# A hand-ordered transformer kernel: value products and scores side by side on TensorE, the sum of p ahead of the scaling of o on VectorE

## The chip, the cores and the metric

One core of a Trainium2 chip runs the whole program. Time is the device time of that core in microseconds (us). The core's engines work from queues of their own and meet only at semaphores: TensorE (PE; PEld is its weight load), VectorE (DVE), ScalarE (ACT), GpSimd (POOL) and SyncE (SP), which only issues DMAs.

## The reference, cut to what matters

```python
x = x + tanh(g_xattn) * xattn(layernorm(x), ctx)              # once, 4 x 512 tokens of 128
x = x + tanh(g_ffn) * body(layernorm(x))
def body(x):
    for i in range(6):
        q, k, v = split(shift_tokens(x) @ Wqkv[i])            # 16 heads of 64
        q, k = rotary(l2norm(q) * q_scale), rotary(l2norm(k) * k_scale)
        sim = q @ k.T * 8, masked to windows of 32 (own and the one before)
        p = exp(sim - max(sim));  o = (p @ v) / sum(p)
        x = o @ Wo[i] + x
        x = (a * gelu(gate)) @ W2[i] + b2[i] + x              # a, gate from layer_norm(shift_tokens(x)) @ W1[i] + b1[i]
    return x
```

All of it is float32.

## The kernel before, in words

After a start of some 50 us (cross attention) the kernel runs the six layers as 192 *units*. A unit is one tile of 128 tokens and one half of the heads (eight heads, 512 columns); eight units make a *group* (one batch element of one layer), four groups a layer, 24 groups in all. The order on each engine is written out by hand as a loop `for n in range(SLOTS)`. A *slot* is one pass n of this loop, `g = n // 8`, `s = n % 8`, and every engine has its own list of steps for a slot, each for an older or newer unit: `queries_keys(n)` beside `scores(n - 3)` and `attend(n - 5)`. So the steps of a unit are spread over seven slots, and the feed-forward work of a group over the slots of the next two groups (`if s == ...`).

TensorE, in a slot: `queries_keys(n)` (L376, q and k of a unit into one of two double banks), `attend(n - 5)` (L448, the value products p v), `values(n)` (L389, v), `transpose_o(n - 6)` (L461), `scores(n - 3)` (L423), `transpose_p(n - 4)` (L436), `transpose_k(n - 2)` (L410), `transpose_q(n - 2)` (L399), and between them by s: `mean` (L498), `fold_bias` (L488, only in the first group of a layer, at s = 2), `variance` (L507), the `up` products (L516), `project_out` (L472, at s = 2 and 6), `down` (L527, at s = 7). `attend` and `scores` consist of 16 small products each, four windows by four pairs of heads, with 32 columns of the array apiece (`tile_position=(0, 32 w)`); every other product uses 128 columns. In the trace a float32 product is two pieces, so such a group is 32 pieces; a transpose is one piece.

Results go to three PSUM banks in turn, the ring: each product calls `turn()` when it is emitted, takes the next bank, and waits until the reader of three turns earlier is done (`ring_read`). So the order in which TensorE's steps stand also sets whose reader each of them waits for. q and k have banks of their own, and so have the scores. `queries_keys(n)` waits for `qn_done` of unit n - 2, which `scale_q(n - 2)` on VectorE gives in the same slot n.

VectorE, in a slot: `sum_p(n - 5)` (L880, the row sums of p), `newton(n - 2)` (L837, L840, L842: three instructions on 128x16, the inverse norms of q and k), `scale_k` (L850) and `scale_q` (L858) of n - 2, `maxima(n - 4)` (L865), `invert_sum(n - 5)` (L888), `less_maxima(n - 4)` (L873), a step by s (among them `centre` at s = 1, L923), `sum_squares(n - 1)` (L824), `clamp_squares(n - 1)` (L830), further steps by s (`add_attention` and `rstd_newton` at s = 3, L907 to L940), `scale_o(n - 5)` (L898, which reads the value products), and after it `layer_norm` (L947, at s = 3, on which the `up` products wait) and `finish` (L978, at s = 1, only for the last four groups).

GpSimd turns k and q of a unit by the rotary tables: six instructions on 128x512 (L1053, L1060, L1096 for k, then L1053, L1060, L1089 for q), started by `scale_k`. ScalarE squares q and k, takes exponentials and copies the ring's banks: v, o, p, k, q (L627, L690, L680, L654, L645). SyncE copies v of a unit into `vw`, once for each window, in eight or ten DMAs, behind the value products of two units before.

Of the kernel before, what the change touches and what calls it, by code (L numbers as in the profile page):

```python
# [66 lines left out]
def build(nc, x_in, ctx_in, g_xattn, g_ffn, Wq, bq, Wk, bk, Wv, bv, Wo_x, bo, Wqkv, q_scale, k_scale,  # L67
          Wo, ln_g, ln_b, W1, b1, W2, b2, rope_in, mats_in, mask_in, out):
    ctx = ExitStack()
    with ctx:  # L70
# [211 lines left out]
        def _(pe):  # L282
# [77 lines left out]
            def queries_keys(u):  # L360
                if not 0 <= u < UNITS:
                    return
                g, layer, b, t, half = place(u)
                if u % UPG == 0 and layer == 0:
                    pe.wait_ge(xT_ready, 2 * (b + 1))
                if u == 1:
                    pe.wait_ge(xT_ready, 4)
                if u % UPG == 0 and layer > 0:
                    pe.wait_ge(*evicted("down", g - B))
                if u % (UPG * B) == 0:  # L370
                    pe.wait_ge(w_dma, 16 * 2 * (1 + B * layer))
                pe.wait_ge(qn_done, past(u - 1))
                tok = xT[:, b, t * P:(t + 1) * P]
                for i in range(2):
                    cut = i * INNER + half * UW
                    mm = pe.matmul(QK[u % 2][:, i * UW:(i + 1) * UW], tok, wqkv[:, layer % 2, cut:cut + UW],  # L376
                                   start=True, stop=True)
                mm.then_inc(qk_mm, 1)
# [60 lines left out]
            def attend(u):  # L439
                if not 0 <= u < UNITS:  # L440
                    return
                i = turn("pv", u)
                pe.wait_ge(vw_dma[u % 2], vw_count(u))
                pe.wait_ge(ring_read[i % RINGS], i // RINGS)
                pe.wait_ge(*evicted("p", u))
                for k in range(HP):
                    for w in range(NW):
                        mm = pe.matmul(heads(RING[i % RINGS][WIN * w:WIN * (w + 1), k * P:(k + 1) * P]),  # L448
                                       pT[:, u % 2, k, WIN * w:WIN * (w + 1)],
                                       vw[:, u % 2, w, :, k * DH:(k + 1) * DH], start=True, stop=True,  # L450
                                       tile_position=(0, WIN * w))
                mm.then_inc(ring_made[i % RINGS], 1)
# [88 lines left out]
            for n in range(SLOTS):  # L541
                g, s = n // UPG, n % UPG
                queries_keys(n)
                attend(n - 5)
                values(n)
                transpose_o(n - 6)
                scores(n - 3)
                transpose_p(n - 4)
                if s == 0:
                    mean(g - 2)  # L550
                if s == 2:
                    fold_bias(g - 2)
                if s == 3:
                    up("gate", 1, g - 2, 0)
                    up("gate", 1, g - 2, 2)
                transpose_k(n - 2)
                if s == 1:
                    variance(g - 2)
                if s == 2:
                    project_out(g - 1, 0)  # L560
                if s == 3:
                    up("gate", 1, g - 2, 1)
                    up("a", 0, g - 2, 0)
                if s == 4:
                    up("a", 0, g - 2, 2)
                if s == 5:
                    up("a", 0, g - 2, 1)
                if s == 6:
                    project_out(g - 1, 1)
                if s == 7:  # L570
                    down(g - 2)
                if s == 0:
                    transpose_out(g - 3)
                transpose_q(n - 2)
# [179 lines left out]
        def _(dve):  # L754
# [225 lines left out]

            for n in range(SLOTS):
                g, s = n // UPG, n % UPG
                sum_p(n - 5)
                newton(n - 2)
                scale_k(n - 2)
                scale_q(n - 2)
                maxima(n - 4)
                invert_sum(n - 5)
                less_maxima(n - 4)
                if s == 1:  # L990
                    centre(g - 2)
                if s == 2:
                    add_eps(g - 2)
                if s == 3:
                    add_bias(g - 2)
                if s == 5:
                    gated(g - 2, 2)
                if s == 6:
                    gated(g - 2, 1)
                sum_squares(n - 1)  # L1000
                if s == 0:
                    add_ffn(g - 3)
                clamp_squares(n - 1)
                if s == 3:
                    add_attention(g - 1, 0)
                    rstd_newton(g - 2)
                if s == 7:
                    add_attention(g - 1, 1)
                if s == 4:
                    gated(g - 2, 0)  # L1010
                scale_o(n - 5)
                if s == 3:
                    layer_norm(g - 2)
                if s == 1:
                    finish(g - 3)


        @block.gpsimd
# [238 lines left out]
```

## Time and profile before

| | |
|---|---|
| median of 3 runs | 1823.83 us (1823.41 to 1828.24) |
| the profiled execution | 1824.23 us, span 1822.2 us |
| granted TensorE clock, mean | 0.99 of full speed |
| TensorE busy | 1750.3 us, 96% |
| TensorE weight load busy | 1116.2 us, 61% |
| VectorE busy | 1619.0 us, 89% |
| ScalarE busy | 1327.5 us, 73% |
| GpSimd busy | 1500.4 us, 82% |
| chain that ended last | TensorE 77%, VectorE 13%, GpSimd 5% |

The busy share of TensorE counts pieces whose ends are modelled; how long a step really holds the engine is read from the start of one group of instructions to the start of the next. An instruction's time includes what it waits inside the engine: a 128x16 instruction that takes 0.17 us at one place and 1.14 us at another did not compute for longer.

### The profile page before, as it was taken

To read this page: it belongs to the slowest core of one execution; us is meant where nothing else is said; L and a number is where in the kernel's file an instruction comes from. 1 tells how busy PE (TensorE), PEld (TensorE's weight loads), DVE (VectorE), ACT (ScalarE), POOL (GpSimd) and SP (SyncE) were. 2 spreads that over 40 slices of the span, in tenths; PEclk is the share of its full clock that TensorE was granted. 3 is DMA by queue.
4 is the path that set the end of the run, shared out by engine and by line. 5 is a ranking of instruction groups with operands and counts; after the bars stand their busy time and mean duration, and the time that the engine had idled before them with its cause. 6 is when DMAs were issued, how large, how long until landed. Compare 5 with 4: busy or idle time off the path is not lost.

```text
span 1822.2 us, 48666 instructions
## 1 busy us (share of the span) xinstructions
PE 1750.3 (96%) x18122; PEld 1116.2 (61%) x18122; DVE 1619.0 (89%) x2782; ACT 1327.5 (73%) x2362; POOL 1500.4 (82%) x1204
## 2 busy tenths in 40 slices
PE   7699999999999999999999999999999999999986
PEld 6356666666666666666666666666666666666663
DVE  7799998999999989989999999899999998988874
ACT  3577877877778778778777777787776877877763
POOL 4799888888888888988888888888888888888860
PEclk9999999999999999999999999999999999999998
DMA  4132222222222222322223222222222222222221
GB/s 114 28 87 67 68 71 57 60 73 76 71 63 69 63 66 71 76 65 68 63 56 81 72 70 72 54 63 73 75 72 62 68 58 58 59 71 56 56 64 29
DMA packets 155273, 120.59 MB, mean 66 GB/s; under 512 B 42607, under 2 KB 151457, under 8 KB 154913
## 3 DMA queue, kind: packets, MB, share of 16 engines
q1 hardware_dynamic: 155041, 117.48, 25.1%
q8 instruction: 147, 2.41, 0.6%
q14 instruction: 85, 0.70, 0.1%
HBM read 18.79 MB, written 1.05 MB: 11 GB/s over the span
## 4 chain that ended last, share of the span: by engine, by line
PE 77%; DVE 13%; POOL 5%; issue 3%; SPq 1%; ACT 1%; DMA 1%; DVEq 0%; POOLq 0%; ACTq 0%
PE qk_bank L376 17%; PE ring_bank L448 10%; PE ring_bank L472 9%; PE ring_bank L389 8%; PE sc_bank L423 7%; PE ring_bank L516 6%; PE ring_bank L436 4%; PE ring_bank L399 3%; PE ring_bank L527 3%; PE ring_bank L461 3%; PE ring_bank L410 3%; DVE rn L842 2%; DVE step L837 2%; DVE o L898 2%; DVE qkn L858 2%
## 5 line engine op out<-in xcount | busy, mean ns | idle before, releaser
L1053 POOL TENSOR_TENSOR turned<-qkn,tables 128x512 f32<-128x512 f32 x384 | 489.3, 1274 | 209.8 <-DVE qkn L850 201.5
L1060 POOL TENSOR_TENSOR turned<-qkn,tables 128x512 f32<-128x512 f32 x384 | 496.7, 1294 | 0.0
L376 PE MATMUL qk_bank<-wqkv,xT 128*128 128x512 f32 x768 | 366.5, 600 | 18.8 <-DVE qkn L858 18.6
L1089 POOL TENSOR_TENSOR turned<-turned 128x512 f32<-128x512 f32 x192 | 255.0, 1328 | 15.1
L1096 POOL TENSOR_TENSOR turned<-turned 128x512 f32<-128x512 f32 x192 | 245.1, 1277 | 15.1
L448 PEld LDWEIGHTS ring_bank<-vw,pT 128*32 128x32 f32 x6144 | 156.6, 110 | 143.8 <-issue 143.7
L654 ACT ACTIVATE kB<-ring_bank 64x512 f32<-64x512 f32 x384 | 225.3, 587 | 23.5 <-PE ring_bank L410 21.2
L824 DVE TENSOR_REDUCE ss<-sq 128x16 f32<-128x1024 f32 x192 | 232.0, 1208 | 6.8 <-ACT sq L618 6.8
L627 ACT ACTIVATE vs<-ring_bank 128x512 f32<-128x512 f32 x192 | 114.7, 598 | 163.1 <-PE ring_bank L389 153.4
L898 DVE TENSOR_TENSOR o<-ring_bank,rr 128x512 f32<-128x512 f32 x192 | 132.1, 688 | 104.2 <-PE ring_bank L448 101.3
L389 PE MATMUL ring_bank<-wqkv,xT 128*128 128x512 f32 x384 | 216.1, 645 | 1.6 <-DVE x L978 1.6
L664 ACT ACTIVATE sc_bank<-mask_f 128x512 f32<-128x512 f32 x192 | 114.5, 596 | 136.0 <-DVE pr L873 135.6
L448 PE MATMUL ring_bank<-vw,pT 128*32 128x128 f32 x6144 | 208.4, 276 | 0.1
L423 PE MATMUL sc_bank<-kB,qT 128*32 128x128 f32 x6144 | 207.5, 276 | 0.3
L376 PEld LDWEIGHTS qk_bank<-wqkv,xT 128*128 128x128 f32 x768 | 131.2, 191 | 121.7 <-issue 93.4
L618 ACT ACTIVATE sq<-qk_bank 128x1024 f32<-128x1024 f32 x192 | 198.0, 1031 | 0.0
L423 PEld LDWEIGHTS sc_bank<-kB,qT 128*32 128x32 f32 x6144 | 156.0, 109 | 34.7 <-issue 34.7
L472 PE MATMUL ring_bank<-oT,wo 128*128 128x256 f32 x768 | 173.8, 379 | 0.0
L461 PEld LDWEIGHTS ring_bank<-ident,o 128*128 128x128 f32 x768 | 95.5, 141 | 102.1 <-issue 83.9
L472 PEld LDWEIGHTS ring_bank<-oT,wo 128*128 128x128 f32 x768 | 142.2, 190 | 18.1 <-DVE uT L956 0.8
L516 PE MATMUL ring_bank<-xnT,w 128*128 128x512 f32 x288 | 143.3, 609 | 8.5 <-DVE xnT L947 7.3
L850 DVE TENSOR_TENSOR qkn<-qk_bank,rn 128x512 f32<-128x512 f32 x192 | 132.9, 692 | 20.7 <-DVE rn L842 0.9
(169 smaller groups left out, 3129.3 us busy)
## 6 DMA issues: line engine op xcount, KB each, us to landing
vw<-vs SPq DMA_DIRECT2D x1152, 64.0 KB, 2.1
vw<-vs SPq DMA_DIRECT2D x672, 32.0 KB, 1.9
wqkv<-in_L_ffn_Wqkv_dram SPq DMA_DIRECT2D x20, 384.0 KB, 3.5
wo<-in_L_ffn_Wo_dram SPq DMA_DIRECT2D x20, 128.0 KB, 3.3
w<-in_L_ffn_W_dram SPq DMA_DIRECT2D x6, 341.0 KB, 3.4
wqkv<-in_L_ffn_Wqkv_dram SPq DMA_DIRECT2D x1, 1536.0 KB, 9.5
x<-in_x_dram SPq DMA_DIRECT2D x2, 512.0 KB, 4.7
out_dram<-x SPq DMA_DIRECT2D x4, 256.0 KB, 2.3
```

The costliest lines, as they stand in the source:

```text
L376: mm = pe.matmul(QK[u % 2][:, i * UW:(i + 1) * UW], tok, wqkv[:, layer % 2, cut:cut + UW], start=True, stop=True)
L389: pe.matmul(RING[i % RINGS][:, :], xT[:, b, t * P:(t + 1) * P], wqkv[:, layer % 2, cut:cut + UW], start=True, stop=True).then_inc(ring_mad ...
L423: mm = pe.matmul(heads(SC_BANK[WIN * w:WIN * (w + 1), k * P:(k + 1) * P]), qT[:, u % 2, k, WIN * w:WIN * (w + 1)], kB[:, HP * half + k, :, ...
L448: mm = pe.matmul(heads(RING[i % RINGS][WIN * w:WIN * (w + 1), k * P:(k + 1) * P]), pT[:, u % 2, k, WIN * w:WIN * (w + 1)], vw[:, u % 2, w, ...
L472: mm = pe.matmul(RING[i % RINGS][:, 0:HALF], wo[:, layer % 2, k, :], oT[:, k, HALF * h:HALF * (h + 1)], start=(k == 0), stop=(k == KO - 1))
L516: pe.matmul(RING[i % RINGS][:, :], w1[:, DFF * j + k * P:DFF * j + (k + 1) * P], xnT[:, :], start=True, stop=True).then_inc(ring_made[i % ...
L654: ev = act.activation(kB[64 * h:64 * h + 64, HP * half:HP * half + HP, h, WIN + P * t:WIN + P * t + P], RING[i % RINGS][64 * h:64 * h + 64 ...
L824: dve.tensor_reduce(ss[:, :], heads(sq[:, :]), AX.X, ALU.add).then_inc(ss_done, 1)
L1053: return pool.tensor_tensor(heads(turned[:, u % 2, 2 * i, :]), heads(qkn[:, u % 2, i * UW:(i + 1) * UW]), table.unsqueeze(1).to_broadcast( ...
L1060: return pool.tensor_tensor(halves(turned[:, u % 2, 2 * i + 1, :]), halves(qkn[:, u % 2, i * UW:(i + 1) * UW])[:, :, ::-1, :], table.rearr ...
L1089: pool.tensor_tensor(q, q, turned[:, u % 2, 1, :], ALU.add).then_inc(q_summed, 1)
L1096: pool.tensor_tensor(k, k, turned[:, u % 2, 3, :], ALU.add).then_inc(k_summed, 1)
```

## The change

On TensorE `values(n)` moves ahead of `attend(n - 5)`, and `scores(n - 3)` ahead of `transpose_o(n - 6)`. On VectorE the row sum moves from the start of a slot to the end of the slot before, ahead of `scale_o` (hence `sum_p(n - 4)`), and `finish` from the end of slot s = 1 to a place ahead of `centre`. No instruction is added or removed.

```diff
@@ TensorE, the loop over slots
                 queries_keys(n)
+                values(n)
                 attend(n - 5)
-                values(n)
+                scores(n - 3)
                 transpose_o(n - 6)
-                scores(n - 3)
                 transpose_p(n - 4)
@@ VectorE, the loop over slots
             for n in range(SLOTS):
                 g, s = n // UPG, n % UPG
-                sum_p(n - 5)
                 newton(n - 2)
...
                 less_maxima(n - 4)
                 if s == 1:
+                    finish(g - 3)
                     centre(g - 2)
...
                 if s == 4:
                     gated(g - 2, 0)
+                sum_p(n - 4)
                 scale_o(n - 5)
                 if s == 3:
                     layer_norm(g - 2)
-                if s == 1:
-                    finish(g - 3)
```

TensorE in slot 4 of a group, from q and k on. Before (x16 are the small products of 32 columns):

```order
L376 MATMUL qk_bank<-wqkv,xT 128x512 x2
L448 MATMUL ring_bank<-vw,pT 32x128 x16
L389 MATMUL ring_bank<-wqkv,xT 128x512
L461 MATMUL ring_bank<-ident,o 128x128 x4
L423 MATMUL sc_bank<-kB,qT 32x128 x16
L436 MATMUL ring_bank<-ident,pr 128x128 x4
L410 MATMUL ring_bank<-ident,turned 128x128 x4
```

And in the changed kernel:

```order
L376 MATMUL qk_bank<-wqkv,xT 128x512 x2
L389 MATMUL ring_bank<-wqkv,xT 128x512
L448 MATMUL ring_bank<-vw,pT 32x128 x16
L423 MATMUL sc_bank<-kB,qT 32x128 x16
L461 MATMUL ring_bank<-ident,o 128x128 x4
L436 MATMUL ring_bank<-ident,pr 128x128 x4
L410 MATMUL ring_bank<-ident,turned 128x128 x4
```

The two groups of 32-column products, which had v and o between them, now stand together.

VectorE at the end of slot 3 and the start of slot 4, before (rstd is the normaliser's inverse deviation, xnT its output):

```order
L938 TENSOR_TENSOR dsq<-dsq,xnT 128x512
L940 SCALAR_TENSOR_TENSOR rstd<-dsq,rstd 128x512
L898 TENSOR_TENSOR o<-ring_bank,rr 128x512
L947 SCALAR_TENSOR_TENSOR xnT<-dT,cols,rstd 128x512
L880 TENSOR_REDUCE rs<-pr 128x8
L837 SCALAR_TENSOR_TENSOR step<-seed 128x16
```

And in the changed kernel:

```order
L938 TENSOR_TENSOR dsq<-dsq,xnT 128x512
L940 SCALAR_TENSOR_TENSOR rstd<-dsq,rstd 128x512
L880 TENSOR_REDUCE rs<-pr 128x8
L898 TENSOR_TENSOR o<-ring_bank,rr 128x512
L947 SCALAR_TENSOR_TENSOR xnT<-dT,cols,rstd 128x512
L837 SCALAR_TENSOR_TENSOR step<-seed 128x16
```

The row sum (L880) stood behind layer_norm (L947) and now stands ahead of both it and scale_o (L898).

## Rows read from the trace of the kernel before

**Rows 1.** The page (busy time), and the view of waits, VectorE.

```profile
PE 1750.3 (96%) x18122; PEld 1116.2 (61%) x18122; DVE 1619.0 (89%) x2782; ACT 1327.5 (73%) x2362; POOL 1500.4 (82%) x1204
DVE o L898 <- PE ring_bank L448: 101.3, 100, 3.6
```

**Rows 2.** Timeline, TensorE, slot 0 of group 11: start, us, engine, line, op, operands.

```profile
818.67 1.88 PE L376 MATMUL qk_bank<-wqkv,xT 128*128 128x512 f32 x4
820.48 1.08 PE L448 MATMUL ring_bank<-vw,pT 128*32 128x128 f32 x32
821.49 1.12 PE L389 MATMUL ring_bank<-wqkv,xT 128*128 128x512 f32 x2
822.46 0.60 PE L461 MATMUL ring_bank<-ident,o 128*128 128x128 f32 x4
822.99 1.08 PE L423 MATMUL sc_bank<-kB,qT 128*32 128x128 f32 x32
...
824.49 1.02 PE L498 MATMUL ring_bank<-xT,mean_w 128*128 128x512 f32 x2
825.35 0.60 PE L410 MATMUL ring_bank<-ident,turned 128*128 128x128 f32 x4
...
826.23 1.88 PE L376 MATMUL qk_bank<-wqkv,xT 128*128 128x512 f32 x4
```

**Rows 3.** Timeline, TensorE: starts of slots 2 to 6 and 8; a fold_bias.

```profile
834.33 1.98 PE L376 MATMUL qk_bank<-wqkv,xT 128*128 128x512 f32 x4 [0.39 <-DVE qkn L858]
...
844.58 1.88 PE L376 MATMUL qk_bank<-wqkv,xT 128*128 128x512 f32 x4
...
855.02 1.88 PE L376 MATMUL qk_bank<-wqkv,xT 128*128 128x512 f32 x4
...
862.58 1.88 PE L376 MATMUL qk_bank<-wqkv,xT 128*128 128x512 f32 x4
...
870.81 1.98 PE L376 MATMUL qk_bank<-wqkv,xT 128*128 128x512 f32 x4 [0.52 <-DVE qkn L858]
...
890.33 1.88 PE L376 MATMUL qk_bank<-wqkv,xT 128*128 128x512 f32 x4
...
1055.41 1.40 PE L488 MATMUL ring_bank<-cols,w 128*128 128x1 f32 x12
```

**Rows 4.** Timeline, VectorE and GpSimd, second half of slot 5.

```profile
865.63 0.69 DVE L898 TENSOR_TENSOR o<-ring_bank,rr 128x512 f32<-128x512 f32 x1
...
866.84 1.14 DVE L837 SCALAR_TENSOR_TENSOR step<-seed 128x16 f32<-128x16 f32 x1
...
868.22 1.14 DVE L842 SCALAR_TENSOR_TENSOR rn<-step,seed 128x16 f32<-128x16 f32 x1
869.46 0.69 DVE L850 TENSOR_TENSOR qkn<-qk_bank,rn 128x512 f32<-128x512 f32 x1
...
866.66 1.28 POOL L1060 TENSOR_TENSOR turned<-qkn,tables 128x512 f32<-128x512 f32 x1
868.02 1.30 POOL L1089 TENSOR_TENSOR turned<-turned 128x512 f32<-128x512 f32 x1
870.30 1.27 POOL L1053 TENSOR_TENSOR turned<-qkn,tables 128x512 f32<-128x512 f32 x1 [0.97 <-DVE qkn L850]
```

**Rows 5.** Timeline, VectorE and GpSimd, in slot 2.

```profile
837.63 0.68 DVE L898 TENSOR_TENSOR o<-ring_bank,rr 128x512 f32<-128x512 f32 x1
...
838.82 0.16 DVE L837 SCALAR_TENSOR_TENSOR step<-seed 128x16 f32<-128x16 f32 x1
...
840.49 0.69 DVE L850 TENSOR_TENSOR qkn<-qk_bank,rn 128x512 f32<-128x512 f32 x1
...
838.86 1.28 POOL L1060 TENSOR_TENSOR turned<-qkn,tables 128x512 f32<-128x512 f32 x1
```

**Rows 6.** Timeline, VectorE and TensorE, layer_norm in slot 3.

```profile
849.44 1.05 DVE L947 SCALAR_TENSOR_TENSOR xnT<-dT,cols,rstd 128x512 f32<-128x512 f32 x1
...
850.64 1.96 PE L516 MATMUL ring_bank<-xnT,w 128*128 128x512 f32 x4
```

## Prediction

> **What bounds the kernel now.** I read the page, then TensorE's timeline over one group, then the timelines of VectorE and GpSimd over its tight places. I call one pass of the unit loop a slot, numbered 0 to 7 in a group, and count inside a slot from the start of its q and k product. The page [rows 1] shows three engines nearly full: TensorE at 96%, VectorE at 89%, GpSimd at 82%. VectorE waited 101.3 us for the value products [rows 1], 4.2 us in each of 24 groups: all the slack that it has.
>
> TensorE issues without a gap through slot 0 of group 11 [rows 2]: q and k at 0, value products at 1.81, v at 2.82, o at 3.79, scores at 4.32, then p, mean at 5.82, next slot at 7.56. The slots of the group last 7.56, 8.10, 10.25, 10.44, 7.56, 8.23, then 19.52 for two [rows 2, 3]: 71.66 us, and 24 such groups make nearly the whole time. The start of slot 2 waited 0.39 and that of slot 6 0.52 for VectorE's scaled q (L858) [rows 3]. So TensorE is full except where a loop through VectorE closes late: value products, scale_o, sum_p, newton, scale_k, scale_q, and then the next slot's q and k, which need the bank that scale_q has read. It is this loop that makes slot 1 8.10 and slot 5 8.23 where slots 0 and 4, with as much work for TensorE, take 7.56.
>
> Matmul busy time may mislead, so I put a page's rule against it. The Trainium skill (Perfetto Trace Analysis, Identifying the Most-Contended Engine) judges TensorE by weight loading instead. By that, with 61% [rows 1] against VectorE's 89%, VectorE is the engine to relieve, and an edit that leaves its work unchanged gives nothing. The starts above have no holes to fill, so I keep TensorE as one bound; the rule is rival "same" below.
>
> **TensorE: fewer changes of shape.** Value products and scores use 32 columns of the array, all else 128. One such group spreads its 32 starts over 1.08 less one piece of 0.27, 0.81 us, so 32 steps are 0.83; it holds TensorE for 1.01 [rows 2], so leaving the shape costs 0.18. After it v takes 0.96 where mean, of the same size, takes 0.86: 0.10. Before it q and k take 1.81 where twice 0.86 is 1.72: 0.09. Side by side, the two groups save one entry and one exit: 0.37 a slot, 192 times, 71 us if TensorE bound everywhere. TensorE's own work becomes 7.19 in slots 0, 1, 4, 5; 9.9 in 2 and 6; 9.77 in 3; 8.91 in 7.
>
> **The loop.** v in front delays the value products by 0.86 us. scale_o began 3.05 after the slot's start (862.58, 865.63 [rows 3, 4]); now 3.91, or 4.02 when q and k started late, with the 0.10 that such a start adds. In exchange sum_p leaves the loop. scale_o and sum_p together take 1.19 [rows 5], so 0.60 leaves and 0.86 enters: 0.26 longer, where the loop already decides slots 1 and 5. Its new place is 0.6 us earlier; I take it that the exponentials, which follow the subtracted maxima on ScalarE while VectorE sums squares, are done by then (bounds: nothing, and its own 0.6).
>
> **What else waits in a new order.** The three ring banks are taken in turn, so who waits for whom changes. The value products now take the bank of the k transposes before (ScalarE's copies into kB), and p takes v's bank, so p now waits for ScalarE's copy of v, which itself waits for the copies to vw of four units ago. Those start behind the value products, so 0.86 later in a slot, and VectorE and the SP queue are not otherwise moved. Behind p stand k and q on TensorE. Bounds: nothing, if v is copied in the two microseconds of value products and scores; 0.5 us in slot 1, behind the shortest slot. VectorE decides slot 1 anyway, so nothing. Scores start at 3.52 instead of 4.32, so 0.8 nearer to ScalarE's copy of q, and behind them stand o and p; that could cost up to 0.3 in a slot that follows a Gelu, slot 4. I take nothing and keep 24 x 0.3 = 7 us for the range. o is turned 0.74 later (4.53), two slots' work ahead of its use in the output product.
>
> **The wait behind GpSimd.** newton is three tiny instructions. In slot 5 it lasts from 866.84 to scale_k at 869.46: 2.62 us, with L837 and L842 each 1.14 [rows 4]. Both end just where a GpSimd instruction ends (868.02; 869.3). In slot 2 L837 starts at 838.82, 0.04 before GpSimd's instruction at 838.86; scale_k comes at 840.49, 1.67 us later [rows 5]. So a tiny instruction gets in at once if it comes in the gap between two GpSimd instructions, and otherwise waits for the end of the one that runs: 0.04 ahead of a start it was in time, 0.18 behind one (866.84, 866.66) it was late. Hence everything hangs on newton's phase against GpSimd. The Trainium skill (GPSIMD Engine Reference, Key points) says that the two engines share SBUF interfaces and contend for instructions of two SBUF inputs; the trace agrees, with the 1.14 above.
>
> In a slot whose start waits for VectorE the phases are fixed: scale_k starts 1.35 before the slot (869.46, 870.81), GpSimd's unit 0.51 before it (870.30) [rows 3, 4]. Its fifth instruction then starts 4.53 after the slot's start (838.86 less 834.33) [rows 3, 5]. Before, scale_o ran at 3.30, when VectorE was free, and newton at 4.49: in the gap. Now VectorE would be ready for scale_o at 3.30 + 0.60 = 3.90, but the value products come at 4.02. newton starts at 4.02 + 0.61 = 4.63, 0.10 behind the fifth instruction's start: **it just misses the gap**. Between the two cases seen, 0.04 ahead and 0.18 behind, 0.10 behind is nearer to the late one, so I take that. It then waits for the end of that instruction and for the whole sixth: scale_k comes as in rows 4, 1.44 after the sixth's start (869.46 less 868.02), which is 1.36 after the fifth's [rows 4]: 4.53 + 1.36 + 1.44 = 7.33. The next slot can start at 7.33 + 1.35 = 8.68. In the gap scale_k would come at 840.49 less 834.33 = 6.16 as in rows 5, and the next slot at 7.51.
>
> **Slots of a common group, forecast.** Slot 0: 3.91 + 0.61 + about 1.65 for newton behind one GpSimd instruction + 1.35 = 7.5. Slot 1: 8.7, before 8.1. Slots 2 and 6: TensorE's 9.9 and 0.1 for the late start, 10.0. Slot 4: 7.2. Slot 5: 8.1, because newton there ended with GpSimd's unit [rows 4], whose place in the slot hardly moves. Slot 7: 8.9. Slot 3: VectorE goes from scale_k at 840.49 to the end of layer_norm at 849.44 + 1.05, 10.0 us [rows 5, 6]; the up products start 0.15 behind it (850.64) and the next slot 4.38 later [rows 3, 6]. sum_p now lies ahead of layer_norm: 10.6, of which I give 0.4 back because layer_norm's 1.05 need not meet GpSimd again; 10.2. With scale_k at 7.33 in a slot of 10.0, layer_norm ends 7.5 into slot 3, which lasts 7.5 + 0.15 + 4.38 = 12.1, before 10.44. Sum: 7.5 + 8.7 + 10.0 + 12.1 + 7.2 + 8.1 + 10.0 + 8.9 = 72.5, against 71.66: +0.85 in 18 groups, +15 us. In the six groups that open a layer, fold_bias adds 12 pieces, some 1.3 us [rows 3], of TensorE's work to slot 2, so VectorE has that lead in slot 3, and I count no change there.
>
> finish moves ahead of centre: four instructions at most. Nearest row: 1.05 [rows 6]; between -4 and +4, taken at -2 since its bank comes free sooner. finish had to go ahead of scale_o, since the value products of that slot now take the bank that finish reads.
>
> From the profiled execution's 1824.2 us (median of the runs 1823.8): 1824 + 15 - 2 = about **1838**.
>
> **Rivals.**
> - *Newton meets the gap in both places* (faster). If the value products arrive 0.1 us sooner than I reckon, slot 1 is 7.5 and slot 3 10.9: a common group 70.1, -1.55 in 18; an opening one about -2.2 in six, as slot 3 gains there too: 1824 - 28 - 13 = 1783. For it: the margin is 0.1 us. Against it: arrival, not VectorE, sets newton, and both terms are from rows.
> - *Gap met in slot 1, missed in slot 2*: slot 1 is 7.5, slot 3 12.1: -0.35 in 18, -1.2 in six: 1811. For it: slot 0 does not start late.
> - *TensorE binds everywhere* (faster): 1824 - 71 = 1753. Against it: VectorE's slack is 4.2 us a group and its waits behind GpSimd grow as slots shrink.
> - *Same*: VectorE's unchanged work sets the pace, the rule above; 1824.
> My forecast is itself the slower side; it decides from the point where newton falls behind the start of GpSimd's fifth instruction. With the 7 us of slot 4 and 4 for finish on top it gives about 1850.
>
> **Numbers.** Forecast 0.43, gap met twice 0.20, once 0.18, TensorE everywhere 0.05, same 0.14. 0.3% (5.5 us) is about what a measurement can tell from no change. Slower 0.43; same 0.15; faster 0.42. The forecast's own range is 1829 to 1850; the whole range 1784 to 1850.
>
> **What would show it.** Value products and scores together 1.84 us, slot 4 at 7.2: the saving is real. Slot 1 near 8.7 with L837 and L842 both over 1.1 us: the missed gap. Slot 3 above 11 with TensorE waiting for xnT (L947): sum_p in front of layer_norm. Slot 1 at 7.5 and slot 3 under 11 would make the forecast wrong, as would scores waiting for qT.

## The result, and the profile after

The changed kernel took **1868.69 us** (median of 4 runs, 1864.16 to 1871.32) against 1823.62 (four runs) before: a ratio of 1.0239, 95% interval 1.0212 to 1.0266. The forecast had the sign, and a third of the size: +14 (1838) against +45, outside its range. The profiled execution took 1871.32 us, its span is 1869.3, 47.1 more than before.

The page of the changed kernel (span, busy time, chain that ended last), which answers to [rows 1]:

```profile
span 1869.3 us, 48666 instructions
...
PE 1741.2 (93%) x18122; PEld 1137.8 (61%) x18122; DVE 1638.4 (88%) x2782; ACT 1316.0 (70%) x2362; POOL 1503.7 (80%) x1204
...
PE 51%; DVE 27%; SPq 7%; ACT 6%; issue 5%; DMA 3%; POOL 0%; DVEq 0%; ACTq 0%
```

TensorE has less to do (1741.2 us, before 1750.3), VectorE more (1638.4, before 1619.0), though not one instruction was added; the chain that ended last runs over VectorE for 27% where it was 13%. The view of waits (us in total, times, longest):

```profile
DVE o L898 <- PE ring_bank L448: 93.7, 142, 2.5
...
ACT vs L627 <- DMA vw<-vs: 46.7, 56, 1.9
...
PE ring_bank L516 <- DVE xnT L947: 35.6, 23, 5.1
...
PE ring_bank L399 <- ACT pT L680: 24.1, 77, 0.4
...
PE qk_bank L376 <- DVE qkn L858: 13.1, 23, 3.2
```

Before, ScalarE's copy of v (L627) waited 8.8 us for the DMAs, the up products (L516) 7.3 us for xnT, and the q transposes (L399) 1.0 us in all for ScalarE's copy of p. VectorE's slack in front of the value products hardly moved, 101.3 [rows 1] to 93.7.

**The shape saving is real.** TensorE's timeline over slot 4 of group 13, which answers to [rows 2]:

```profile
1031.26 1.88 PE L376 MATMUL qk_bank<-wqkv,xT 128*128 128x512 f32 x4
1032.98 1.02 PE L389 MATMUL ring_bank<-wqkv,xT 128*128 128x512 f32 x2
1033.93 1.08 PE L448 MATMUL ring_bank<-vw,pT 128*32 128x128 f32 x32
1034.83 1.06 PE L423 MATMUL sc_bank<-kB,qT 128*32 128x128 f32 x32
1035.81 0.66 PE L461 MATMUL ring_bank<-ident,o 128*128 128x128 f32 x4
...
1038.62 0.66 PE L399 MATMUL ring_bank<-ident,turned 128*128 128x128 f32 x4 [0.28 <-ACT pT L680]
```

Value products and scores start 0.90 apart, and o follows 0.98 later: 1.88 for the pair, forecast 1.84, before 1.01 for the value products [rows 2] and as much for the scores. What follows q and k (now v, before the value products) starts 1.72 behind them, before 1.81 [rows 2].

**But q waits for the bank of p.** The last row waits. q takes p's bank in both orders: in every slot in which one product of the feed-forward or the output stands beside p, k and q, q is the third turn behind p. What is new is when ScalarE empties that bank. ScalarE in the same slot:

```profile
1036.57 0.60 ACT L690 ACTIVATE oT<-ring_bank 128x512 f32<-128x512 f32 x1 [1.31 <-PE ring_bank L461]
1037.06 1.02 ACT L618 ACTIVATE sq<-qk_bank 128x1024 f32<-128x1024 f32 x1
1037.96 0.60 ACT L680 ACTIVATE pT<-ring_bank 128x512 f32<-128x512 f32 x1
```

ScalarE stood idle for 1.31 us until o was turned, then squared q and k, and copied p only then; the bank came free at 1038.56, and the q transposes, which stand last in the slot, started at 1038.62. The slot lasts 7.86. The same two instructions in slot 4 before (start 855.02):

```profile
861.10 0.60 ACT L680 ACTIVATE pT<-ring_bank 128x512 f32<-128x512 f32 x1
...
862.14 0.60 PE L399 MATMUL ring_bank<-ident,turned 128*128 128x128 f32 x4
```

There p's copy began 6.08 into the slot and ended 0.44 ahead of the q transposes; now it begins at 6.70 and ends only 0.06 ahead of them.

**Newton misses the gap.** VectorE, then GpSimd, at the end of slot 1 (start 1000.95, on time) and in slot 2 (start 1009.24), which answer to [rows 4, 5]:

```profile
1005.48 0.93 DVE L837 SCALAR_TENSOR_TENSOR step<-seed 128x16 f32<-128x16 f32 x1
...
1006.65 1.14 DVE L842 SCALAR_TENSOR_TENSOR rn<-step,seed 128x16 f32<-128x16 f32 x1
1007.90 0.69 DVE L850 TENSOR_TENSOR qkn<-qk_bank,rn 128x512 f32<-128x512 f32 x1
...
1013.87 1.23 DVE L837 SCALAR_TENSOR_TENSOR step<-seed 128x16 f32<-128x16 f32 x1
...
1015.34 1.13 DVE L842 SCALAR_TENSOR_TENSOR rn<-step,seed 128x16 f32<-128x16 f32 x1
1016.58 0.69 DVE L850 TENSOR_TENSOR qkn<-qk_bank,rn 128x512 f32<-128x512 f32 x1
...
1013.79 1.28 POOL L1059 TENSOR_TENSOR turned<-qkn,tables 128x512 f32<-128x512 f32 x1
1015.15 1.30 POOL L1088 TENSOR_TENSOR turned<-turned 128x512 f32<-128x512 f32 x1
```

In slot 2 newton starts 4.63 behind the slot's start (1009.24, 0.27 late), 0.08 behind GpSimd's fifth instruction; scale_k (L850) starts at 7.34, where it was 6.16 [rows 3, 5]. In slot 1 newton is late too, by 0.4, and scale_k at 6.95 makes the slot 8.29. Slot 3 (TensorE starts 1019.30) pays for slot 2; VectorE and TensorE, which answer to [rows 6]:

```profile
1024.67 0.67 DVE L880 TENSOR_REDUCE rs<-pr 128x8 f32<-128x512 f32 x1
...
1025.98 0.74 DVE L947 SCALAR_TENSOR_TENSOR xnT<-dT,cols,rstd 128x512 f32<-128x512 f32 x1
...
1026.87 1.96 PE L516 MATMUL ring_bank<-xnT,w 128*128 128x512 f32 x4 [1.71 <-DVE xnT L947]
```

**In the first two groups nearly every slot is caught.** There no feed-forward work fills the slots. The first five last as before; from slot 5 of group 0 on each is long, until one with an output product comes (slot 2 of group 1), and behind that it begins again. TensorE (three q and k products on end), then VectorE in the slot between the second and the third:

```profile
106.68 1.98 PE L376 MATMUL qk_bank<-wqkv,xT 128*128 128x512 f32 x4 [0.70 <-DVE qkn L858]
...
115.45 1.95 PE L376 MATMUL qk_bank<-wqkv,xT 128*128 128x512 f32 x4 [0.80 <-DVE qkn L858]
...
124.02 1.98 PE L376 MATMUL qk_bank<-wqkv,xT 128*128 128x512 f32 x4 [0.71 <-DVE qkn L858]
...
120.05 1.15 DVE L837 SCALAR_TENSOR_TENSOR step<-seed 128x16 f32<-128x16 f32 x1
...
121.44 1.12 DVE L842 SCALAR_TENSOR_TENSOR rn<-step,seed 128x16 f32<-128x16 f32 x1
122.67 0.69 DVE L850 TENSOR_TENSOR qkn<-qk_bank,rn 128x512 f32<-128x512 f32 x1
```

A slot that starts late misses the gap, so the next starts late, and so on: 8.55 to 8.77 us a slot for as long as nothing breaks the cycle, where before such slots took 7.65 to 7.67 and the one at s = 7 8.34.

**Where the 47 us are.** Median slot lengths in a common group, and their sum:

| slot | 0 | 1 | 2 | 3 | 4 | 5 | 6 | 7 | sum |
|---|---|---|---|---|---|---|---|---|---|
| before | 7.56 | 8.10 | 10.25 | 10.45 | 7.56 | 8.22 | 10.25 | 9.28 | 71.67 |
| forecast | 7.5 | 8.7 | 10.0 | 12.1 | 7.2 | 8.1 | 10.0 | 8.9 | 72.5 |
| after | 7.86 | 8.29 | 10.06 | 11.95 | 7.86 | 7.86 | 9.96 | 9.11 | 72.95 |

Slot 3 alone is 1.50 longer, slots 0 and 4 0.30 each, slot 1 0.19; slots 2, 5, 6 and 7 are 1.01 shorter together. Slot 3, which pays for slot 2's missed gap, is the largest part of a common group's 1.28.

By stretches: up to the first q and k product 51.3 us before and 57.5 after; groups 0 to 2, 192.0 and 202.7; groups 3 to 22, 1436.8 and 1462.5; the rest +4.5. The first of these, +6.2, isn't the change's: what runs there is the same, but the granted TensorE clock was not. The window from 30 to 40 us, before and then after (the third figure from the end is the clock as a share of full speed):

```profile
30.00:40.00 10.00, 8.94 (x81) 8.75 (x79) 6.33 (x19) 2.66 (x5) 1.27 (x2) 1.00 0.16 14
30.00:40.00 10.00, 10.00 (x49) 10.00 (x48) 2.77 (x4) 2.08 (x4) 0.00 (x0) 0.50 0.18 14
```

Of the 17 profiles here nine have 1.00 in this window and reach the first q and k product at 51.3 to 53.1 us; the other eight have 0.50 to 0.56 and reach it at 56.0 to 58.0.

### The profile page after: what moved, and what is told of

It is laid out like the page before. It is cut to its first block, busy times and chain, and to the rows that moved or that the text cites. A ratio compares the mean times of both kernels' runs of the same rounds, so it can differ in the third digit from the quotient of the medians.

```text
span 1869.3 us, 48666 instructions
## 1 busy us (share of the span) xinstructions
PE 1741.2 (93%) x18122; PEld 1137.8 (61%) x18122; DVE 1638.4 (88%) x2782; ACT 1316.0 (70%) x2362; POOL 1503.7 (80%) x1204
## 4 chain that ended last, share of the span: by engine, by line
PE 51%; DVE 27%; SPq 7%; ACT 6%; issue 5%; DMA 3%; POOL 0%; DVEq 0%; ACTq 0%
PE qk_bank L376 11%; PE ring_bank L448 7%; PE ring_bank L389 5%; PE ring_bank L472 5%; PE ring_bank L516 5%; PE sc_bank L423 4%; SPq L1180 4%; PE ring_bank L399 3%; DVE ss L824 3%; DVE rn L842 3%; DVE step L837 3%; PE ring_bank L461 3%; ACT sq L618 3%; DVE o L898 3%; PE ring_bank L527 3%
## 5 line engine op out<-in xcount | busy, mean ns | idle before, releaser
L690 ACT ACTIVATE oT<-ring_bank 128x512 f32<-128x512 f32 x192 | 114.7, 597 | 210.9 <-PE ring_bank L461 210.0
L898 DVE TENSOR_TENSOR o<-ring_bank,rr 128x512 f32<-128x512 f32 x192 | 132.9, 692 | 95.7 <-PE ring_bank L448 93.7
L423 PE MATMUL sc_bank<-kB,qT 128*32 128x128 f32 x6144 | 203.6, 273 | 1.3 <-ACT qT L645 1.3
L389 PE MATMUL ring_bank<-wqkv,xT 128*128 128x512 f32 x384 | 198.5, 599 | 0.0
L516 PE MATMUL ring_bank<-xnT,w 128*128 128x512 f32 x288 | 149.7, 632 | 35.6 <-DVE xnT L947 35.6
L472 PE MATMUL ring_bank<-oT,wo 128*128 128x256 f32 x768 | 178.7, 386 | 0.0
L423 PEld LDWEIGHTS sc_bank<-kB,qT 128*32 128x32 f32 x6144 | 172.1, 110 | 3.9 <-issue 3.8
L399 PEld LDWEIGHTS ring_bank<-ident,turned 128*128 128x128 f32 x768 | 86.8, 141 | 134.6 <-ACT pT L680 84.0
L627 ACT ACTIVATE vs<-ring_bank 128x512 f32<-128x512 f32 x192 | 113.5, 591 | 69.6 <-DMA vw<-vs 46.7
L399 PE MATMUL ring_bank<-ident,turned 128*128 128x128 f32 x768 | 121.0, 280 | 42.9 <-ACT pT L680 24.1
```

What stands on the lines that cost most here:

```text
L389: pe.matmul(RING[i % RINGS][:, :], xT[:, b, t * P:(t + 1) * P], wqkv[:, layer % 2, cut:cut + UW], start=True, stop=True).then_inc(ring_mad ...
L399: mm = pe.transpose(RING[i % RINGS][:, k * P:(k + 1) * P], turned[:, u % 2, 0, k * P:(k + 1) * P], ident[:, :])
L423: mm = pe.matmul(heads(SC_BANK[WIN * w:WIN * (w + 1), k * P:(k + 1) * P]), qT[:, u % 2, k, WIN * w:WIN * (w + 1)], kB[:, HP * half + k, :, ...
L472: mm = pe.matmul(RING[i % RINGS][:, 0:HALF], wo[:, layer % 2, k, :], oT[:, k, HALF * h:HALF * (h + 1)], start=(k == 0), stop=(k == KO - 1))
```

## The experiments

The account so far was: newton's phase against GpSimd (slots 1, 3 and the first groups), ScalarE's copies (slots 0, 4, 5), the row sum ahead of layer_norm (slot 3). Against it stood that the v product in front costs what its 0.86 us say and the phase is only a symptom, or that the pair of 32-column groups itself does harm. The table gives the two kernels and the 15 made for this; "20 groups" is the time of groups 3 to 22 in the profiled execution, free of the start and the first groups. The ratio is to the kernel before, run on the same chip, where it took 1823.57 to 1829.08; so rows whose medians lie within some 6 us of each other are compared by the ratios or the 20 groups.

| kernel | median us | ratio (95%) | 20 groups, us |
|---|---|---|---|
| before | 1823.62 | 1 | 1436.8 |
| after | 1868.69 | 1.0239 (1.0212 to 1.0266) | 1462.5 |
| sum_back | 1873.52 | 1.0253 (1.0233 to 1.0273) | 1467.6 |
| v_alone | 1869.68 | 1.0234 (1.0214 to 1.0254) | 1464.4 |
| squares_first | 1862.31 | 1.0188 (1.0165 to 1.0212) | 1455.1 |
| ln_first | 1865.51 | 1.0209 (1.0185 to 1.0232) | 1460.2 |
| pair_early | 1854.03 | 1.0150 (1.0135 to 1.0165) | 1462.7 |
| pair_early_sq | 1826.67 | 0.9997 (0.9982 to 1.0011) | 1439.2 |
| no_newton_before | 1794.80 | 0.9826 (0.9810 to 0.9842) | 1409.6 |
| no_newton_after_sq | 1815.12 | 0.9933 (0.9911 to 0.9956) | 1424.2 |
| no_newton_v_alone | 1801.22 | 0.9864 (0.9841 to 0.9888) | 1412.4 |
| sq_vs7 | 1863.13 | 1.0204 (1.0178 to 1.0230) | 1455.4 |
| no_newton_before_vs7 | 1789.13 | 0.9798 (0.9772 to 0.9823) | 1404.8 |
| no_newton_after_sq_vs7 | 1750.10 | 0.9591 (0.9565 to 0.9616) | 1371.1 |
| newton_early | 1822.24 | 0.9983 (0.9967 to 0.9998) | 1427.6 |
| newton_early_before | 1903.16 | 1.0424 (1.0402 to 1.0446) | 1496.7 |
| newton_early_ln | 1820.40 | 0.9971 (0.9955 to 0.9986) | 1427.0 |

### Which part of the change

**sum_back**: the changed kernel with the row sum back at the start of the slot.

```diff
+                sum_p(n - 5)
                 newton(n - 2)
...
-                sum_p(n - 4)
                 scale_o(n - 5)
```

> The changed kernel with sum_p back at the start of a slot, behind scale_o. My theory: slots 1 and 2 are held by newton's waits for GpSimd, which swallow sum_p, so they stay at 8.3 and 10.0; slots 0, 4 and 5 are held by ScalarE (q transposed into the bank of p) and stay at 7.86; only slot 3 gains, 0.6 us, because layer_norm comes 0.6 us sooner: group 72.4 instead of 72.95, about 1855 us. Rival (sum_p in front of scale_o pays as such, hidden in the wait for the value products): slots 0, 1, 4, 5 grow by up to 0.6 each and the time rises to 1880 or more.

1873.52 us, slots summing to 73.22: by the slots the row sum's new place is worth 0.3 in a group, which the ratios of the whole time (1.0253 and 1.0239) do not tell apart. The 14 us expected from moving it back did not come. Back in its old place it cost 0.30, 0.10 and 0.19 in slots 5, 6 and 7 and gave 0.29 in slot 3. The loop is 0.6 longer than in the changed kernel, yet slots 1 and 2 did not move.

**v_alone**: sum_back, and the pair parted again, so that of the change only v in front is left (and finish).

```diff
                 queries_keys(n)
                 values(n)
                 attend(n - 5)
-                scores(n - 3)
                 transpose_o(n - 6)
+                scores(n - 3)
```

> The kernel before with v ahead of the value products only (scores stay behind o; sum_p as before; finish ahead of centre, which this order needs). TensorE changes shape as often as before. My theory: this is the cost of the delay alone: slots 0 and 4 7.55, slot 1 8.3, slot 2 10.25, slot 3 11.6 (layer_norm late), slots 5 to 7 as before: group 72.8, about 1845 us. Rival (the delay costs nothing, all of the loss is the later o and scores): 1824.

1869.68 us, where 1845 was expected: v in front (with `finish`, which that order needs) makes the whole loss. Its sum is 73.05, slots 1 and 3 take 8.51 and 11.50. The pair on top of it, in sum_back, gave nothing (73.22): TensorE did not set the slots that were long.

**pair_early**: the kernel before with scores behind the value products, both ahead of v.

```diff
                 queries_keys(n)
                 attend(n - 5)
+                scores(n - 3)
                 values(n)
                 transpose_o(n - 6)
-                scores(n - 3)
```

> The kernel before with scores directly behind the value products and both ahead of v: one change of shape fewer, the value products not delayed, sum_p as before. Theory (the loss of the change is the delay of the value products; the side by side itself saves 0.37 a slot): slots 1, 2, 3 lose their excess over before, but scores come at 2.7 and wait up to 0.6 us for ScalarE's copy of q in slots 1, 2, 4, 6, and o is turned at 4.7, so ScalarE holds the q transposes as in the changed kernel and slots 0, 4 and 5 last about 7.9 to 8.0: 1825 to 1840 us. Rival (scores beside value products cost by themselves): 1860 or more.

1854.03 us, above the 1840 expected and slower than before too, without v in front of the value products. Its waits name another engine, the same as in slot 4 above:

```profile
ACT vs L627 <- PE ring_bank L389: 370.8, 190, 3.6
...
PEld ring_bank L399 <- ACT pT L680: 85.3, 88, 1.1
```

ScalarE waits for v in nearly every slot, and its squares, and behind them the norms, queue behind that copy.

### ScalarE and layer_norm

**squares_first**: the changed kernel, ScalarE's squares ahead of its copy of o.

```diff
                 copy_v(n)
-                copy_oT(n - 6)
                 squares(n)
+                copy_oT(n - 6)
```

> The changed kernel with ScalarE's squares(n) ahead of copy_oT(n-6). My theory: slots 0, 4 and 5 last 7.86 because o is turned 0.74 later, so oT is copied at 5.31, squares follow to 6.8, and p's copy, whose bank the q transposes take, ends at 7.3. With squares ahead p's copy ends near 6.3: slots 0 and 4 fall to 7.2 to 7.5, slot 5 to 7.5 to 8.1 (VectorE behind GpSimd), group 71.9 to 72.3, about 1845 to 1855 us. Rival (the copies to vw or VectorE hold these slots): they stay at 7.86 and the time at 1869.

1862.31 us. TensorE's q transposes no longer wait for p (of the 84.0 us that their weight loads waited 18.8 are left), and slots 0 and 4 are 7.45 and 7.36. But slot 1, which now starts late, is 8.68, the very slot that had been forecast. It started at 991.58, on TensorE; VectorE, GpSimd and the start of slot 2:

```profile
996.48 0.97 DVE L837 SCALAR_TENSOR_TENSOR step<-seed 128x16 f32<-128x16 f32 x1
...
997.69 1.13 DVE L842 SCALAR_TENSOR_TENSOR rn<-step,seed 128x16 f32<-128x16 f32 x1
998.93 0.69 DVE L850 TENSOR_TENSOR qkn<-qk_bank,rn 128x512 f32<-128x512 f32 x1
...
996.14 1.27 POOL L1059 TENSOR_TENSOR turned<-qkn,tables 128x512 f32<-128x512 f32 x1
997.49 1.30 POOL L1088 TENSOR_TENSOR turned<-turned 128x512 f32<-128x512 f32 x1
1000.27 0.70 PE L376 MATMUL qk_bank<-wqkv,xT 128*128 128x512 f32 x1 [0.39 <-DVE qkn L858]
```

newton at 4.90, scale_k at 7.35, next slot at 8.69. Of 0.91 us gained in slots 0 and 4, 0.39 was given back in slot 1, 0.10 in slot 6 and 0.18 in slot 7.

**ln_first**: the changed kernel, in slot 3 alone the row sum behind layer_norm.

```diff
-                sum_p(n - 4)
+                if s != 3:
+                    sum_p(n - 4)
                 scale_o(n - 5)
                 if s == 3:
                     layer_norm(g - 2)
+                    sum_p(n - 4)
```

> The changed kernel with sum_p behind scale_o and layer_norm in slot 3 only. My theory: the up products wait for layer_norm, so slot 3 falls by 0.6 us from 11.96 to 11.35 in common groups and by less in the ones that open a layer; nothing else moves: 1857 us. Rival (slot 3 is long because of GpSimd's hold on rstd_newton alone): less than 0.2 us, 1866.

1865.51 us. Slot 3 went from 11.95 to 11.66, not by the 0.6 of the row sum: layer_norm, ahead of it, lasted 1.04 where it had lasted 0.74, beside a GpSimd instruction again. Slots 5, 6 and 7 took back 0.05, 0.10 and 0.19. The rest of slot 3 (before 10.45) is scale_k of slot 2.

**pair_early_sq**: pair_early, and the squares ahead of both copies.

```diff
+                squares(n)
                 copy_v(n)
                 copy_oT(n - 6)
-                squares(n)
```

> The same with ScalarE's squares(n) ahead of copy_v and copy_oT, so that the late v and o do not hold them. Theory: slots 0 and 4 about 7.3, slot 1 8.1, slots 2 and 6 9.95, slot 3 10.7, slot 5 8.2, slot 7 9.0: group 70.5, about 1796 us, faster than both kernels. Rival (VectorE and GpSimd set the pace whatever TensorE saves): 1824.

1826.67 us, no difference from before and 30 over what was expected; the slots sum to 71.65. Slots 0, 1, 3 and 5 are 0.15 to 0.5 shorter than before, slots 2, 4 and 6 0.4 to 0.5 longer. There the scores, which stand right behind the value products now, wait for ScalarE's copy of q (27.5 us in all). TensorE in slot 2 (start 980.51):

```profile
983.91 1.08 PE L423 MATMUL sc_bank<-kB,qT 128*32 128x128 f32 x32 [0.40 <-ACT qT L645]
```

So the pair needs something ahead of the scores, and v is what the change puts there. The two orders trade one wait for another.

### Without newton

Five kernels leave newton out: the inverse norms of q and k are used as ScalarE gives them, without the refinement step (L837, L840, L842; for each of these kernels, that is the part of the computation that is missing). They take away what is disturbed by GpSimd inside the loop, 0.5 us of work in each slot and up to 2.6 with its waits.

```diff
-                newton(n - 2)
...
-                dve.wait_ge(rn_done, u + 1)
+                dve.wait_ge(seed_done, u + 1)
...
-spread(rn[:, u % 2, HU:], DH)
+spread(seed[:, u % 2, HU:], DH)
```

**no_newton_before**: this edit to the kernel before.

> The kernel before without newton: scale_k and scale_q take the seed of the inverse norm as it is, so three tiny VectorE instructions a slot and their waits for GpSimd are left out. Theory (newton's waits for GpSimd close the loop in slots 1 and 5 and lengthen slot 3): slots 1 and 5 fall to 7.6, slot 3 to 10.13, TensorE full: group 70.0, 1785 us. Rival (they are hidden): 1824.

1794.80 us, 1.7% off: slots 1 and 5 fall to 7.55, slot 3 to 10.13, slots 2 and 6 lose 0.1, and the others stay. TensorE now sets nearly every slot: in the 20 groups three waits are left, 1.7 us together.

**no_newton_v_alone**: this edit to v_alone.

> v ahead of the value products only, as v_alone, and newton left out. Theory: the 41 us that v_alone lost were newton missing the gap between GpSimd's instructions; without newton nothing of it is left but slot 3, where layer_norm may hold the up products by some tenths: 1795 to 1802 us, as no_newton_before. Rival (the delay costs through another path, the copies or the ring): 1815 or more.

1801.22 us, where no_newton_before has 1794.80: by the ratios v in front costs 0.4% without newton, and 2.3% with it. So its 0.86 us in the loop cost little by themselves. This run alone doesn't part newton's phase from newton's own 0.5 us, which leave the loop with it; sum_back does, where 0.6 us more in the loop left slots 1 and 2 as they were, and newton_early below.

**no_newton_after_sq**: this edit to squares_first.

> The changed kernel without newton and with squares ahead of copy_oT. Theory: with both holders gone (GpSimd's hold on newton, ScalarE's late copy of p) TensorE's saving shows: slots 0 and 4 7.3, 1 and 5 7.65 (GpSimd's six instructions), 2, 3 and 6 9.9, 7 9.1: group 68.7, 1752 us, faster than the kernel before without newton by 30 us. Rival (delaying the value products costs by something else): not faster than that one.

1815.12 us, 63 over what was expected and slower than no_newton_before, though TensorE has less to do. Slots 1, 3 and 6 were long, 8.73, 10.33 and 10.90. ScalarE and TensorE in slot 1 of group 13 (start 972.05):

```profile
977.47 0.60 ACT L627 ACTIVATE vs<-ring_bank 128x512 f32<-128x512 f32 x1 [1.73 <-DMA vw<-vs]
...
978.12 0.66 PE L436 MATMUL ring_bank<-ident,pr 128*128 128x128 f32 x4 [0.86 <-ACT vs L627]
```

ScalarE's copy of v waits until the DMAs of an older unit have left the buffer, and p waits for v's bank. That is the wait which the prediction had named and put at nothing.

### The copies to vw

`vs`, from which SyncE copies v, gets a seventh buffer.

```diff
-VS = 6
+VS = 7
...
-                    act.wait_ge(vw_dma[u % 2], vw_count(u - VS + 2))
+                    act.wait_ge(vw_dma[(u - VS + 2) % 2], vw_count(u - VS + 2))
```

**no_newton_after_sq_vs7**: this edit to no_newton_after_sq.

> The changed kernel without newton, squares ahead of copy_oT, seven buffers of v. Theory: all three holders gone (newton behind GpSimd, late copy of p, copies to vw): slots 0 and 4 7.2 to 7.4, 1 and 5 about 7.7 (GpSimd's six instructions), 2 and 6 9.9, 3 10.3 (layer_norm), 7 9.1: group 69.4, 1775 us, some 20 us under the kernel before without newton. Rival: not under it.

1750.10 us, 65 less. TensorE has no gap left in slot 1 (start 931.54):

```profile
936.59 0.60 PE L436 MATMUL ring_bank<-ident,pr 128*128 128x128 f32 x4
937.02 0.60 PE L410 MATMUL ring_bank<-ident,turned 128*128 128x128 f32 x4
937.50 1.13 PE L507 MATMUL ring_bank<-dsq,mean_w 128*128 128x512 f32 x2
...
938.90 0.59 PE L376 MATMUL qk_bank<-wqkv,xT 128*128 128x512 f32 x1
```

The slot lasts 7.36, and the group 68.25.

**no_newton_before_vs7**: the control, both edits to the kernel before.

> The kernel before without newton and with seven buffers of v: the control. Its copies of v wait for the copies to vw but nobody waits for them, TensorE is full: no change against no_newton_before, 1795 us.

1789.13 us; the medians of its slots sum to the same 69.92 as without the buffer, and what the 20 groups lost (1409.6 to 1404.8) were single longer slots. Between this kernel and the last stands the change with the squares moved, and nothing else: 39 us by the medians, 1.67 in a group of eight slots, 33.7 over the 20 groups. In the two profiles 6.2 of the 40.8 us between them are the start's clock (0.50 and 1.00 from 30 to 40 us), so some 35 us, 1.9%, are the change's. That is what the change is worth where VectorE and ScalarE let TensorE run: 0.34 in slot 0 and 0.17 to 0.20 in the others, against 0.37 forecast. All slots save 0.34 until k is turned (5.48, before 5.82). In slot 0 that stays; where a 512-column product stands behind k, as in the last rows, it holds TensorE for 0.96 (937.50, next 938.46) where it was 0.86 before, and k itself for 0.48 instead of 0.44. No run explains these 0.14.

**sq_vs7**: squares_first with the seventh buffer and with newton.

> The changed kernel with squares ahead of copy_oT and a seventh buffer for v, so that copy_v waits for the copies to vw of five units ago instead of four. Theory (two holders gone, GpSimd's hold on newton stays): slots 0 and 4 7.4, slot 5 7.9, slots 1, 2 and 3 still 8.3 to 8.7, 10.0 and 11.9, since their loop never waited for the copies; group 72.6, 1860 us, no more than 5 us under squares_first. Rival (the copies behind the value products are what the delay costs): 1835 or less.

1863.13 us, as squares_first (1862.31). With newton in the loop the copies cost nothing, though 46.7 us of waits are put down to them in the profile after.

### Another place for newton

**newton_early**: sq_vs7, newton of the next unit ahead of scale_o, where VectorE had waited for the value products.

```diff
-                newton(n - 2)
...
                 sum_p(n - 4)
+                newton(n - 1)
                 scale_o(n - 5)
```

> The changed kernel with squares ahead of copy_oT, seven buffers of v, and newton kept whole but moved ahead of scale_o (for unit n-1), so out of the loop that the value products close. If the place of newton is the cost: its waits for GpSimd overlap the wait for the value products; scale_k comes 5.0 to 6.2 into a slot instead of 5.2 to 7.3; slots 0, 1, 4, 5 7.3 to 7.6, group 69 to 71, 1765 to 1810 us, faster than the kernel before. If its presence is the cost (0.7 us of VectorE and its waits, which only move in front of scale_o and still delay it): as sq_vs7, 1850 or more.

1822.24 us, 41 less than sq_vs7 with all its work, by the ratios 2.2% for the place of three instructions. What is left to no_newton_after_sq_vs7, 72 us, is the work and its waits. VectorE and TensorE in slot 2 (start 981.87):

```profile
985.95 1.20 DVE L840 TENSOR_TENSOR step<-step,ssm 128x16 f32<-128x16 f32 x1
...
987.30 0.69 DVE L898 TENSOR_TENSOR o<-ring_bank,rr 128x512 f32<-128x512 f32 x1
...
988.04 0.66 PE L410 MATMUL ring_bank<-ident,turned 128*128 128x128 f32 x4 [0.52 <-DVE o L898]
```

newton is still stretched by GpSimd, now in front of scale_o, which starts at 5.43; k, which takes the value products' bank, waits for it.

**newton_early_before**: the same move in the kernel before.

> The kernel before with only newton moved ahead of scale_o (for unit n-1). If the place of newton is the cost: slots 1 and 5 fall to 7.6 as TensorE is full there, group 70.0 to 70.8, 1790 to 1805 us. But here the value products come at 3.05, when the seed is not yet there (ScalarE gives it at about 3.5), so newton may hold scale_o by a microsecond: then it is no faster than before, 1824.

1903.16 us. In that order the value products come 0.86 earlier, so newton, which waits for ScalarE's seeds, stands in scale_o's way, and p waits for scale_o's bank:

```profile
PE ring_bank L436 <- DVE o L898: 88.6, 128, 1.3
```

The change's order of TensorE and this place of newton go together: of the two orders with newton early, the changed one is 4.2% faster (it also has the squares and the buffer moved), and with newton in its old place 2.0% slower (sq_vs7 against before). No run has newton early and the squares moved in the order of before, so part of the 4.2% may be theirs.

**newton_early_ln**: newton_early, and in slot 3 row sum and newton behind layer_norm.

```diff
                 scale_o(n - 5)
                 if s == 3:
                     layer_norm(g - 2)
+                    sum_p(n - 4)
+                    newton(n - 1)
```

> newton_early with sum_p and newton behind layer_norm in slot 3 alone. There layer_norm ended 6.6 into the slot and the up products waited 1.1 us for it. Theory: layer_norm then ends at 5.3, the up products do not wait, slot 3 falls from 11.13 to 9.95 in 18 groups and by 0.4 in the others: 24 us less, about 1800 us, faster than both kernels by over 1%. Rival (the loop gets the time back in slot 4 or 5, as newton now ends at 6.5): 1815 or more.

1820.40 us, 0.29% under before (0.14% to 0.45%): with newton_early, from which its ratio doesn't part it, the fastest with all arithmetic, and 20 over what was expected. Slot 3 gained 1.28 in a common group (9.85, newton_early 11.13), slots 4 and 5 gave back 0.9 of it, and in the six opening groups slot 2 rose to 13.6, so that the 20 groups took 1427.0 us against 1427.6.

## Why the prediction was right in sign and wrong in size

- **Shape saving.** Forecast 0.37 a slot from one entry and one exit, and up to the turn of k it is 0.34. Too large was the saving in the term "TensorE's own work becomes 7.19": 7.36 in slots 1, 4 and 5, since 0.14 comes back behind k; so 0.19 was left of 0.37 in seven slots of eight. That entry and exit cost 0.37 fits the starts, but was not measured by itself.
- **Missed gap.** Right, with its numbers: newton at 4.63, scale_k at 7.33 forecast and 7.34 measured. newton_early bears it out as the cost: newton's place alone moved the time by 2.2%. The choice between "in time" and "late" at 0.10 need not have been a guess: the trace before has eight of newton's instructions that start 0.10 to 0.14 behind a GpSimd instruction's start, and all lasted 1.16 to 1.21. The 868.02 read as a GpSimd instruction's end is the next one's start (that one ended at 867.94), which changes nothing. Two places were off: in a common group slot 1 starts on time (slot 0 is long for another reason), so it is 8.29; the 8.68 stands in squares_first.
- **Slot 3.** 12.1 forecast, 11.95 measured, by way of slot 2. The row sum's part in it was 0.3, not 0.6.
- **The exponentials** were taken as done when the row sum comes. Once a group, in slot 4, they weren't: VectorE waited for them 1.15 us in group 13, 26.1 us in all. It cost nothing, for scale_o then waited 0.62 more for the value products.
- **"What else waits in a new order"** is the first step that failed, at the term "o is turned 0.74 later (4.53), two slots' work ahead of its use", which it put at nothing. o's use is not what hurts: ScalarE stands still until o is turned and takes the squares and p's copy behind it, so p's copy comes 0.62 later (6.70, before 6.08), and q, which takes p's bank in either order, waits for it. The list of new pairs was wrong besides: it is v, not the value products, that takes the bank of the k transposes in most slots, and k now takes the value products' bank, a wait for scale_o that the prediction does not have and that cost nothing here (in newton_early 34.7 us). Slots 0, 4 and 5 were put at 7.5, 7.2 and 8.1 and all take 7.86: +0.78 a group. With -0.41 in slot 1 and +0.08 elsewhere, a common group is 72.95 against 72.5.
- **The sum over groups** is the second. It took 18 common groups and six of "no change". The six came out 0.5 longer. Above all, groups 0 and 1 have no work between the steps of a slot, so the missed gap feeds itself in every one: groups 0 to 2 took 10.6 more, where the sum had 1.7. The mechanism was in the prediction; that it has no exit there was not.
- **Outside the loop**: +6.2 at the start, which goes with the clock (1.00 and 0.50 between 30 and 40 us), and +3.4 behind the last q and k product instead of the -2 for finish. The end was not taken apart further.
- Together: forecast +13 (15 less 2) in the profiled execution; +9 for groups 0 to 2, +13 for groups 3 to 22 (25.7 against 15 x 0.85; the medians give 22 of the 25.7, single longer slots the rest), +12 for the start, the last group and the end: 47.
- **p behind the copies to vw** was rightly put at nothing for this kernel, since with newton in the loop the seventh buffer changed nothing; without newton it was 65 us.
- **The rivals.** Both "gap met" fell with newton's 4.63. "TensorE binds everywhere" fell with slots 1 and 3: TensorE is 51% of the chain that ended last, before 77%. "Same", by which VectorE is the engine to relieve as its share is above the 61% of weight loading (the Trainium skill, Perfetto Trace Analysis, Identifying the Most-Contended Engine), fell as well: the same work in another order moved the time by 2.4%. With newton and the waits gone, weight loading has 65% and GpSimd 86%, yet TensorE issues without a gap, and the chain that ended last is 91% TensorE's.

## What to carry to other kernels

When a step is moved in a hand-written order, work out for each product whose reader it now waits for, and for each short instruction beside GpSimd where it falls between that engine's starts; a loop that closes on itself can lock into the worse phase and stay there. Look for the stretches with nothing to break such a cycle, and price them apart from the common one. A saving on one engine is worth its size only after the others have been moved out of its way: the same order of TensorE gave +2.4% as it was, -0.2% with newton, the squares and a buffer moved, and some -2% where newton was left out on both sides.

## What the runs showed of the hardware

- The edge of the gap is narrow. In the trace before, all 152 of newton's 128x16 instructions that started 0.05 to 0.01 us ahead of the start of a GpSimd instruction on 128x512 took 0.16 to 0.18 us. One that started with it took 1.31. Those that started 0.04 or more behind it lasted until 0.03 or 0.04 past its end (1.27 us for the one at 0.04), or their own 0.16 where less was left. The Trainium skill (GPSIMD Engine Reference, Key points) says that the two engines contend; these rows say for how long.
- So time put ahead of such an instruction is not simply added: in sum_back 0.6 us was put into the loop and a group grew by 0.27, slots 1 and 2 not at all.
- The same instructions ahead of the loop took 51.3 to 53.1 us in the nine profiles in which the granted TensorE clock was 1.00 (2.4 GHz) between 30 and 40 us, and 56.0 to 58.0 in the eight with 0.50 to 0.56 (about 1.2 GHz). Two single profiles can differ by that much, whatever the change.
